# Cross-attention and gated FFN on one core: K, Q and V moved behind the first square layer, whose first three groups advance in step behind the gates

## The chip, the cores and the metric

The kernel runs on one core of a Trainium2 chip. Its five engines work side by side and meet at semaphores: TensorE (PE: matmuls, and PEld: the loading of their weights), VectorE (DVE), ScalarE (ACT), GpSimd (POOL) and SyncE (SP), which issues nearly all DMAs. The metric is the device time of one launch in microseconds (us), lower is better, as the median of several runs.

## The reference

32 sequences of 128 tokens, width 256, each with a context of 128 tokens of width 512.

```
xn  = layernorm(x)
kv  = (ctx @ W_src.T + b_src) * mask          # 512 -> 2*256: keys, values
q   = (xn  @ W_tgt.T + b_tgt) * mask          # 256 -> 256, 8 heads of 32
p   = softmax(where(mask, q @ k.T / sqrt(32), -inf))
x   = x + concat(xn, p @ v) @ W_out.T + b_out
h   = layernorm(x)
h   = silu((h @ w1.T) * s1) * ((h @ w2.T) * s2)   # 256 -> 1024, the gates
h   = gelu((h @ h1.T) * s3)                       # 1024 -> 1024, first square layer
h   = gelu((h @ h2.T) * s4)                       # 1024 -> 1024, second square layer
out = x + (h @ w3.T) * s5                         # 1024 -> 256
```

The weights of the FFN are whole numbers from -1 to 1. All data are float32.

## The kernel before, in words

**Tiles.** The 4096 tokens are cut into 16 tiles of two sequences (256 columns). Three tiles are under way at a time: while the FFN of tile f runs, tile a = f + 1 is in the second half of its attention (softmax normalised, transposed by a DMA round trip, weighted sums, output projection, second layer norm), tile n = f + 2 gets its K, Q, V and scores, and for tile m = f + 3 data are loaded and the first layer norm is done. Tile 0, and tiles 13, 14 and 15, are written out; tiles 1 to 12 are passes of a loop (`Fori`) that each engine has for itself. Each engine works through its own list in program order and waits at semaphores; there is no scheduler, so the order in which the helpers are called is the order of the work.

**Two operand halves.** The square layers and gates are computed as a high half (float32 rounded, "fp32r", line 780 in the square layers and 686 in the gates) and a low half (float16 with the high 16 bits of the weights, lines 778 and 685). Every activation is therefore split by DVE (`split`, lines 1379 to 1403) into `hAh`/`hAq` or `hBh`/`hBq`. K, Q, V, scores, weighted sums and output projection are plain float32 (lines 534, 552, 570, 588, 660, 677).

**PE's order in one pass f.** `gates_part` has four groups of gates (`gate_up`, q = 0 to 3, banks G0/G1 and F0/F1 in turn), then `project_k` twice, `project_q` and `project_v` of tile n. `middle_part` has the first square layer as q = 4 to 7 and the second as q = 8 to 11, in banks F0 and F1 in turn; each q has two halves of 128 output columns, and each half 8 high and 8 low products. Ahead of q = 8 stand `attend(a)`, `scores(n)` and `out_proj(a)`. Then comes `ffn_out`. In tiles 14 and 15 alone q = 4, 5, 6 are done by `middle_three`: the first halves of all three advance together, over k = 0 to 3, then 4 and 5, then 6 and 7, with the third group in G0, and the second halves follow. There the first square layer stands directly behind the gates, since no K, Q and V are left to compute.

**What feeds it.** ACT takes each gate bank through silu (`silu`, line 952), then has 16 exponentials of tile a, then the gelus (line 961) of q = 4 to 11. DVE multiplies gate by up (`gate_times_up`, line 1376), splits, adds bias and mask to K, Q and V (lines 1172, 1184, 1191), masks scores, normalises (1223), transposes 32 x 32 blocks (1277), and makes the two halves of the FFN's input from `x2T`: `x2h` by ACT and, in `x2_lo` (line 1343), the float16 `x2q` and a second low half `x2l`. `x2l` is read by PE only in a branch (`general`) for weights with low bits, which is not taken with these inputs. POOL has in tile 0 the rounding of the weights (`cast`, line 1623), which the second square layer of tile 0 waits for chunk by chunk, and the powers for the layer norms (1583, 1595).

**Tile 0** has an order of its own in DVE's list: `mask_scores(1, 0)` stands between `split(0, 0)` and `gate_times_up(0, 1)`, and the first layer norm of tile 3 (`ln1_apply`, which waits for POOL) stands ahead of `split(0, 10)`.

Of the kernel before, what the change touches and what calls it, by code (L numbers as in the profile page):

```python
# [12 lines left out]
NB = 2  # L13
# [30 lines left out]
def program(nc, x, ctxT, mask_row, mask_col, wsT, wvT, wtT, woT, first_rows, second_rows, x_mask_1, w1T, w2T, h1T, h2T,  # L44
            w3T, out):
    st = ExitStack()
    with st:
# [129 lines left out]
        def mid_bank(f, q):  # L177

            if q in (6, 10) and isinstance(f, int) and (f == TILES - 1 or f in (0, TILES - 2) and q == 6):
                return G[0][:].rearrange("p (h t) -> p h t", h=2)  # L180
            return F[q % 2][:]
# [172 lines left out]
        def _(sp):  # L354
# [43 lines left out]
            def turn_x2(a):  # L398
                sp.wait_ge(xt2_ready, at("xt2_ready", a - 1, 2))
                if not isinstance(a, int) or a > 1:  # L400
                    sp.wait_ge(x2T_loaded, at("x2T_loaded", a - 2, 64))
                sp.dma_start(x2_dram.rearrange("q p n -> p q n"), xt2[:].rearrange("p q c j i -> p q (c j i)")).then_inc(x2_written, 16)
                sp.wait_ge(x2_ready, at("x2_ready", a - 1, 2))
                sp.wait_ge(x2f_ready, at("x2f_ready", a - 1, 2))
                sp.wait_ge(x2_written, at("x2_written", a - 1, 16))
                for q in range(ROWS):
                    sp.dma_start(x2T[q * DH:(q + 1) * DH].rearrange("p a c j i -> p a (c j i)"),
                                 x2_dram[q].rearrange("(a b) n -> b a n", b=DH)).then_inc(x2T_loaded, 16)
# [14 lines left out]
            def tile(f, a, m):  # L423
                if m is not None:
                    load_ctx(m)
                    load_mask_row(m)
                if a is not None:
                    write_p(a, 0)
                    write_p(a, 1)
                    read_p(a, 0)  # L430
                    read_p(a, 1)
                if m is not None:
                    load_mask_col(m)
                    load_x(m)
                if a is not None:
                    turn_x2(a)
                if is_first(f):
                    spread_lift()
                if m is not None:
                    turn_x(m)  # L440
                store(f)
# [61 lines left out]
        def _(pe):  # L503
# [34 lines left out]
            def project_q(a, cs=range(KD), ks=range(KD)):  # L538
                by_dma = not isinstance(a, int) or a > 2
                if by_dma:  # L540
                    pe.wait_ge(xT_loaded, at("xT_loaded", a - 3, 64))
                    pe.wait_ge(sil_ready, at("sil_ready", a - 2, KH - 2))
                else:
                    pe.wait_ge(xnT_ready, at("xnT_ready", a, 1))
# [148 lines left out]

            def gate_group(bank, W, cols, lows, general):

                for low in lows:
                    for k in range(KD):
# [4 lines left out]
            def gate_up(f, q, general):  # L702

                gate_bank, up_bank = gate_banks(q)
                pe.wait_ge(x2_ready, at("x2_ready", f, 2))
                if general:
                    pe.wait_ge(x2f_ready, at("x2f_ready", f, 2))
                if q == 1 and isinstance(f, int) and f == 0:
# [5 lines left out]
                for h in range(2):  # L714
                    cols = slice((2 * q + h) * P, (2 * q + h + 1) * P)
                    ins = gate_group(gate_bank[:, h, :], (W1, W1_raw), cols, (h == 1, h == 0), general)
                ins.then_inc(gate_done, 1)
# [8 lines left out]
                for h in range(2):  # L726
                    cols = slice((2 * q + h) * P, (2 * q + h + 1) * P)
                    ins = gate_group(up_bank[:, h, :], (W2, W2_raw), cols, (h == 1, h == 0), general)
                ins.then_inc(up_done, 1)

            def middle_bank(f, q):
# [7 lines left out]
                elif q == 6 and isinstance(f, int) and f == 0:  # L739
                    pe.wait_ge(qT_ready, at("qT_ready", 2, 2))  # L740
                elif q == 6 and isinstance(f, int) and f >= TILES - 2:
                    pe.wait_ge(sil_ready, at("sil_ready", f, KH - 2))
                elif q == 7 and isinstance(f, int) and (f == 0 or f >= TILES - 2):
                    pe.wait_ge(gelu_ready, at("gelu_ready", f, 4))
                elif q == 8 and isinstance(f, int) and (f == 0 or f >= TILES - 2):
                    pe.wait_ge(gelu_ready, at("gelu_ready", f, 2))
# [89 lines left out]
            def gates_part(f, a, n, general):  # L836

                first = isinstance(f, int) and f == 0
                for q in range(4):
                    gate_up(f, q, general)  # L840
                    if first and q == 0:
                        scores(1)
                if n is not None:
                    if first:
                        transposes_x(2)
                    project_k(n, 0)
                    project_k(n, 1)
                    project_q(n)
                    project_v(n)

            def middle_part(f, a, n, general):

                first_scores = isinstance(f, int) and f in (0, TILES - 3)
                ends = isinstance(f, int) and f >= TILES - 2
                begun = isinstance(f, int) and f == 0
                for q in range(4, 12):
                    if q == 8 and begun:
                        second_layer_steps(range(KH // 2), general)
                    if q == 8 and first_scores:
                        scores(n)  # L860
# [4 lines left out]
                    if q == 8 and a is not None:  # L865
                        out_proj(a)
                    if ends and q < 7 or a is None and q in (8, 9, 10):
                        if q % 4 == 0:
# [263 lines left out]
        def _(dve):  # L1132
# [205 lines left out]
            def x2_lo(a):  # L1338
                dve.wait_ge(x2hi_ready, at("x2hi_ready", a, 2))
                dve.wait_ge(up_done, at("up_done", a - 1, 4))  # L1340
                for low, ready in ((x2q, x2_ready), (x2l, x2f_ready)):
                    for k in range(KD):
                        V.tensor_tensor(low[:, k, :].rearrange("p (j a i) -> p a j i", j=NB, a=ROWS), x2T[:, :, k],
                                        x2h[:, k, :].rearrange("p (j a i) -> p a j i", j=NB, a=ROWS).bitcast(F32),
                                        ALU.subtract).then_inc(ready, 1)

# [101 lines left out]
            def tile(f, a, n, m):  # L1448
# [6 lines left out]
                gate_times_up(f, 0)  # L1455
                split(f, 0)
                if first:
                    mask_scores(1, 0)
                gate_times_up(f, 1)
                if first:  # L1460
                    gate_times_up(f, 2)
# [14 lines left out]
                if first:  # L1476
                    row_max(1, 1)
                elif n is not None:
                    bias_mask_k(n)
                if n is not None:  # L1480
                    mask_bias(n)
                    bias_mask_q(n)
                if a is not None and not early:
                    normalise(a, 0)
                if n is not None and not first:
                    bias_v(n)
                if a is not None and not early:
# [6 lines left out]
                for q in range(4, 8):  # L1494
                    split(f, q)
                if n is not None:
                    mask_scores(n, 0)
# [13 lines left out]
                if m is not None:  # L1511
                    ln1_stats(m)
                    ln1_apply(m)
                elif n is not None:
                    normalise(n, 0)
                    turn_blocks(n, 0)
                split(f, 10)
                if m is not None:
# [227 lines left out]
```

## Time and profile before

| | |
|---|---|
| median of 3 runs | 896.8 us (896.63 to 896.85) |
| the profiled execution | 897.4 us |
| its span, first to last instruction | 895.6 us |
| granted TensorE clock, mean | 0.999 of full speed |
| PE busy | 889.3 us (99%), 7600 matmuls |
| PEld busy | 817.5 us (91%) |
| DVE busy | 655.5 us (73%) |
| ACT busy | 404.0 us (45%) |
| POOL busy | 79.8 us (9%) |
| DMA | 79.27 MB, mean 89 GB/s |

The profile is of one execution. The span leaves out 1.8 us around the first and the last instruction (897.4 - 895.6). Matmuls overlap in the array: one is shown for longer than the distance to the next, so a busy share of 99% says that PE had work, not how fast it went through it; for that one takes distances between starts, or the chain of waits, which lays the work end to end.

### The profile page before, as it was taken

How to read it: one execution, taken by the hardware profiler on the slowest of the kernel's cores; microseconds unless marked ns; L12 is line 12 of the kernel's file. 1: busy time of each engine (PE TensorE's matmuls, PEld its weight loads, DVE VectorE, ACT ScalarE, POOL GpSimd, SP SyncE). 2: the span in 40 equal slices, each digit the busy share in tenths (PEclk: the TensorE clock that was granted, in tenths of full speed). 3: DMA queues.
4: the chain of work that ended last, by engine and by line, in shares of the span. 5: the costliest groups of instructions: out<-in, count | busy, mean ns of one | idle time of the engine just before them, and what ended most of it. 6: DMA issues, size and time to landing. Idle time of an engine off the chain costs nothing.

```text
span 895.6 us, 20744 instructions
## 1 busy us (share of the span) xinstructions
PE 889.3 (99%) x7600; PEld 817.5 (91%) x7600; DVE 655.5 (73%) x1325; ACT 404.0 (45%) x1125; POOL 79.8 (9%) x109
## 2 busy tenths in 40 slices
PE   9999999999999999999999999999999999999998
PEld 8799899999999999999999999999999999998997
DVE  5897868678686886868768686786867868687463
ACT  5897624435244252533526235262443524455231
POOL 3545000010000100001010010100001000000000
PEclk9999999999999999999999999999999999999999
DMA  9932142412324122142321424113241222303000
GB/s 345 395 106 57 44 117 71 123 47 68 84 65 123 57 85 75 47 123 70 100 58 35 123 70 123 35 46 112 70 123 47 73 84 62 96 24 107 25 13 14
DMA packets 82498, 79.27 MB, mean 89 GB/s; under 512 B 8738, under 2 KB 75042, under 8 KB 82466
## 3 DMA queue, kind: packets, MB, share of 16 engines
q1 hardware_dynamic: 81890, 78.31, 28.2%
q10 hardware_dynamic: 576, 0.52, 0.2%
q8 instruction: 21, 0.34, 0.2%
q14 instruction: 11, 0.09, 0.0%
HBM read 51.55 MB, written 27.26 MB: 88 GB/s over the span
## 4 chain that ended last, share of the span: by engine, by line
PE 92%; DVE 3%; POOL 1%; issue 1%; DMA 1%; ACT 1%; SPq 0%; DVEq 0%; POOLq 0%
PE F L780 24%; PE F L778 22%; PE F L832 6%; PE G L677 6%; PE G L534 5%; PE G L570 5%; PE F L686 3%; PE G L686 3%; PE G L685 3%; PE F L685 3%; PE G L552 3%; PE S L588 2%; PE G L660 2%; PE F L692 1%; PE S L523 1%
## 5 line engine op out<-in xcount | busy, mean ns | idle before, releaser
L961 ACT ACTIVATE g<-F,small 128x256 f32<-128x256 f32 x118 | 49.6, 472 | 199.9 <-PE F L780 199.9
L780 PE MATMUL F<-hBh,H 128*128 128x256 f32 x944 | 131.5, 288 | 0.0
L780 PE MATMUL F<-hAh,H 128*128 128x256 f32 x928 | 130.7, 288 | 0.0
L780 PEld LDWEIGHTS F<-hBh,H 128*128 128x128 f32 x944 | 117.0, 188 | 1.7 <-ACT hBl_raw L961 0.3
L961 ACT ACTIVATE hBl_raw<-F,small 128x256 f32<-128x256 f32 x116 | 48.6, 472 | 155.0 <-PE F L780 155.0
L780 PEld LDWEIGHTS F<-hAh,H 128*128 128x128 f32 x928 | 115.3, 188 | 1.9 <-ACT hAl_raw L952 0.4
L778 PE MATMUL F<-hBq,H 128*128 128x256 f16 x944 | 114.4, 273 | 0.0
L778 PE MATMUL F<-hAq,H 128*128 128x256 f16 x928 | 113.5, 273 | 0.0
L778 PEld LDWEIGHTS F<-hBq,H 128*128 128x128 bf16 x944 | 87.3, 98 | 11.9
L778 PEld LDWEIGHTS F<-hAq,H 128*128 128x128 bf16 x928 | 85.4, 98 | 11.7
L1398 DVE TENSOR_SCALAR hBl_raw<-hBl_raw,small 128x512 f32<-128x512 f32 x60 | 29.2, 486 | 87.3 <-ACT hBl_raw L961 87.3
L988 ACT ACTIVATE pr<-pr,nmx 128x128 f32<-128x128 f32 x240 | 92.6, 387 | 0.5 <-DVE nmx L1216 0.3
L1595 POOL TENSOR_TENSOR rs<-ve,neg_half 128x2 f32<-128x2 f32 x15 | 10.5, 702 | 639.2 <-DVE ve L1326 639.2
L832 PE MATMUL F<-W,hAh 128*128 128x256 f32 x256 | 61.7, 282 | 1.0 <-DVE hAl L1402 0.9
L832 PE MATMUL F<-W,hAl 128*128 128x256 f32 x256 | 61.5, 281 | 0.0
L686 PE MATMUL F<-x2h,W 128*128 128x256 f32 x256 | 51.5, 302 | 0.6 <-DVE g L1376 0.6
L686 PE MATMUL G<-x2h,W 128*128 128x256 f32 x256 | 51.2, 301 | 0.0
L534 PE MATMUL G<-cT,WK 128*128 128x256 f32 x224 | 50.7, 379 | 0.0
L570 PE MATMUL G<-WV,cT 128*128 128x256 f32 x224 | 50.6, 379 | 0.0
L952 ACT ACTIVATE hAl_raw<-G,gscols 128x256 f32<-128x256 f32 x60 | 25.2, 471 | 55.2 <-PE G L686 55.2
L832 PEld LDWEIGHTS F<-W,hAh 128*128 128x128 f32 x256 | 48.3, 189 | 1.4 <-DVE hAl L1402 1.4
L1402 DVE TENSOR_TENSOR hAl<-g,hAh 128x512 fp32r<-128x512 f32 x68 | 47.1, 693 | 2.3
(209 smaller groups left out, 1659.2 us busy)
## 6 DMA issues: line engine op xcount, KB each, us to landing
p_dram<-pb SPq DMA_DIRECT2D x30, 512.0 KB, 3.3
pr<-p_dram SPq DMA_DIRECT2D x120, 128.0 KB, 3.2
H_raw<-h SPq DMA_DIRECT2D x16, 512.0 KB, 13.9
cT<-ctx_t SPq DMA_DIRECT2D x14, 512.0 KB, 3.2
x_dram<-xt SPq DMA_DIRECT2D x28, 256.0 KB, 2.3
out<-y SPq DMA_DIRECT2D x32, 128.0 KB, 1.7
x_in<-x_t SPq DMA_DIRECT2D x15, 256.0 KB, 2.7
x2T<-x_dram SPq DMA_DIRECT2D x60, 64.0 KB, 1.9
```

Source lines behind the costliest of these rows:

```text
L534: ins = mm(k_part(a, c), WK[:, k, c * P:(c + 1) * P], cT_of(a)[:, k, :], start=k == 0, stop=k == KC - 1)
L570: ins = mm(v_bank(a)[:, j * D:(j + 1) * D], cT_of(a)[:, k, j * P:(j + 1) * P], WV[:, k, :], start=k == 0, stop=k == KC - 1)
L677: ins = mm(G[1][:, j * D:(j + 1) * D], lhsT, WO[:, k, :], start=k == 0, stop=k == 2 * KD - 1)
L685: return mm(bank, high_halves(W[0])[:, k, cols], x2q[:, k, :], start=first, stop=last)
L686: return mm(bank, W[0][:, k, cols], x2h[:, k, :], start=first, stop=last)
L778: ins = mm(bank, high_halves(W[0])[:, k, cols], low16[:, k, :], start=first, stop=last)
L780: ins = mm(bank, W[0][:, k, cols], hi[:, k, :], start=first, stop=last)
L832: ins = mm(F[j][:, 0, :], lhsT, W3[:, k, :], start=first, stop=last)
L961: fn(g_pair(f, q)[:, m, :], mid_bank(f, q)[:, m, :], ACT.Gelu, scale=scale).then_inc(gelu_ready, 1)
L988: ins = fn(pr[j][:, r, c, :], pr[j][:, r, c, :], ACT.Exp, bias=nmx[:, j, h:h + 1], scale=SCALE, accum_out=den[:, j, h:h + 1])
L1398: V.tensor_scalar(whole_g, whole_g, lift[:, 1:2], None, ALU.mult).then_inc(in_lift, 1)
L1402: V.tensor_tensor(lo[:, pair, :], whole_g, hi[:, pair, :].bitcast(F32), ALU.subtract).then_inc(h_ready, 1)
```

## The change

1. PE: `project_k`, `project_q` and `project_v` of tile n leave `gates_part` and stand ahead of `attend`, behind q = 7, for every tile but 0.
2. PE: `middle_three` is used for q = 4, 5, 6 in tiles 1 to 13 too; q = 6 is in bank G0 in every tile. The waits on banks follow: q = 6 waits for the silu of q = 2, q = 7 for gelu of 5, q = 8 for gelu of 4, and `project_q` for gelu of 6.
3. DVE: the bias and mask steps of K, Q and V stand behind the splits of q = 4 to 7. The second low half `x2l` is no longer made outside tile 0; the branch that read it multiplies the whole `x2T` instead.
4. DVE, tile 0: `gate_times_up(0, 1)` stands ahead of `mask_scores(1, 0)`, and `split(0, 10)` ahead of `ln1_apply(3)`.
5. SP: the loads of context and mask row of tile m stand behind the DMAs of `p` (outside tile 0).

```diff
@@ mid_bank
-            if q in (6, 10) and isinstance(f, int) and (f == TILES - 1 or f in (0, TILES - 2) and q == 6):
+            if q == 6 or q == 10 and isinstance(f, int) and f == TILES - 1:
                 return G[0][:].rearrange("p (h t) -> p h t", h=2)
@@ SP, turn_x2
-                sp.wait_ge(x2f_ready, at("x2f_ready", a - 1, 2))
+                sp.wait_ge(up_done, at("up_done", a - 1, 4))
@@ SP, tile
-                if m is not None:
+                if is_first(f):
                     load_ctx(m)
                     load_mask_row(m)
...
                     read_p(a, 0)
                     read_p(a, 1)
+                if m is not None and not is_first(f):
+                    load_ctx(m)
+                    load_mask_row(m)
@@ PE, project_q
-                    pe.wait_ge(sil_ready, at("sil_ready", a - 2, KH - 2))
+                    pe.wait_ge(gelu_ready, at("gelu_ready", a - 2, 6))
@@ PE, gates (the branch that is not taken with these inputs)
+            def whole_group(bank, W, cols):
+
+                to = bank.rearrange("p (j a i) -> p j a i", j=NB, a=ROWS)
+                for k in range(KD):
+                    ins = mm(to, W[1][:, k, cols], x2T[:, :, k].rearrange("p a j i -> p j a i"), start=k == 0, stop=k == KD - 1)
+                return ins
...
+                if general and not is_first(f):
+                    return whole_group(bank, W, cols)
@@ PE, middle_bank
-                elif q == 6 and isinstance(f, int) and f >= TILES - 2:
+                elif q == 6:
                     pe.wait_ge(sil_ready, at("sil_ready", f, KH - 2))
-                elif q == 7 and isinstance(f, int) and (f == 0 or f >= TILES - 2):
+                elif q == 7:
                     pe.wait_ge(gelu_ready, at("gelu_ready", f, 4))
-                elif q == 8 and isinstance(f, int) and (f == 0 or f >= TILES - 2):
+                elif q == 8:
                     pe.wait_ge(gelu_ready, at("gelu_ready", f, 2))
@@ PE, gates_part
-                if n is not None:
-                    if first:
-                        transposes_x(2)
-                    project_k(n, 0)
-                    project_k(n, 1)
-                    project_q(n)
-                    project_v(n)
+                if first:
+                    transposes_x(2)
+                    project(2)
+
+            def project(n):
+
+                project_k(n, 0)
+                project_k(n, 1)
+                project_q(n)
+                project_v(n)
@@ PE, middle_part
+                    if q == 8 and n is not None and not begun:
+                        project(n)
...
-                    if ends and q < 7 or a is None and q in (8, 9, 10):
+                    if not begun and q < 7 or a is None and q in (8, 9, 10):
                         if q % 4 == 0:
                             middle_three(f, q, general)
@@ DVE, x2_lo
-                for low, ready in ((x2q, x2_ready), (x2l, x2f_ready)):
-                    for k in range(KD):
...
+                for k in range(KD):
+                    V.tensor_tensor(x2q[:, k, :].rearrange("p (j a i) -> p a j i", j=NB, a=ROWS), x2T[:, :, k],
+                                    x2h[:, k, :].rearrange("p (j a i) -> p a j i", j=NB, a=ROWS).bitcast(F32),
+                                    ALU.subtract).then_inc(x2_ready, 1)
@@ DVE, tile
                 split(f, 0)
+                gate_times_up(f, 1)
                 if first:
                     mask_scores(1, 0)
-                gate_times_up(f, 1)
-                if first:
                     gate_times_up(f, 2)
...
-                elif n is not None:
-                    bias_mask_k(n)
-                if n is not None:
                     mask_bias(n)
                     bias_mask_q(n)
...
-                if n is not None and not first:
-                    bias_v(n)
...
                 for q in range(4, 8):
                     split(f, q)
+                if n is not None and not first:
+                    bias_mask_k(n)
+                    mask_bias(n)
+                    bias_mask_q(n)
+                    bias_v(n)
...
                     ln1_stats(m)
+                    if first:
+                        split(f, 10)
                     ln1_apply(m)
...
-                split(f, 10)
+                if not first:
+                    split(f, 10)
```

## Rows read from the trace of the kernel before

**Rows 1.** The page, part 1: busy time of each engine, share of the span.

```profile
PE 889.3 (99%) x7600; PEld 817.5 (91%) x7600; DVE 655.5 (73%) x1325; ACT 404.0 (45%) x1125; POOL 79.8 (9%) x109
```

**Rows 2.** Busy time by stretch, one pass of the loop (PE, PEld, DVE, ACT, POOL).

```profile
367.68:422.38 54.70, 54.70 (x474) 50.49 (x473) 40.87 (x83) 22.93 (x66) 2.85 (x4) 1.00 0.27 79
```

**Rows 3.** The chain of waits, same pass: start us, us, what.

```profile
375.09 3.45 PE G L534 x16
378.54 1.73 PE G L552 x8
...
383.72 0.93 PE F L780 x8
...
398.26 1.01 PE G L660 x32
399.27 1.10 PE S L588 x32
```

**Rows 4.** Timeline of PE, same pass: start us, us, what [idle before].

```profile
374.61 0.48 PE L686 MATMUL F<-x2h,W 128*128 128x256 f32 x2
...
398.19 1.08 PE L660 MATMUL G<-pr,v 128*32 128x128 f32 x32
```

**Rows 5.** Timeline of PE, tile 14, from the gates' end to `attend`.

```profile
812.20 0.48 PE L686 MATMUL F<-x2h,W 128*128 128x256 f32 x2
...
827.65 0.64 PE L660 MATMUL G<-pr,v 128*32 128x128 f32 x16
```

**Rows 6.** Timeline of PEld, tile 15, at the gates' end.

```profile
858.62 0.53 PEld L780 LDWEIGHTS F<-hAh,H 128*128 128x128 f32 x4 [0.21 <-ACT hAl_raw L952]
```

**Rows 7.** Timeline of DVE, the pass of rows 2.

```profile
378.58 0.88 DVE L1172 SCALAR_TENSOR_TENSOR kT<-G,firsts 128x256 f32<-128x256 f32 x2 [0.37 <-PE G L534]
...
383.92 0.69 DVE L1191 TENSOR_TENSOR vb<-G,firsts 128x512 f32<-128x512 f32 x1 [1.37 <-PE G L570]
...
400.76 1.22 DVE L1208 TENSOR_TENSOR pr<-S,mbias 128x1024 f32<-128x1024 f32 x1
```

**Rows 8.** Timeline of ACT, same pass.

```profile
382.63 1.28 ACT L961 ACT_TABLE_LOAD   x1
387.39 0.84 ACT L961 ACTIVATE hBl_raw<-F,small 128x256 f32<-128x256 f32 x2 [3.48 <-PE F L780]
```

**Rows 9.** Timeline of DVE, tile 0, about the last splits.

```profile
87.04 0.17 DVE L1149 TENSOR_SCALAR ve<-mv 128x2 f32<-128x2 f32 x1
88.04 0.74 DVE L1158 TENSOR_SCALAR xn<-x_in,mv,rs 128x256 f32<-128x256 f32 x2 [0.83 <-POOL rs L1583]
...
89.14 0.69 DVE L1402 TENSOR_TENSOR hAl<-g,hAh 128x512 fp32r<-128x512 f32 x1
...
91.08 0.75 DVE L1343 TENSOR_TENSOR x2l<-x2T,x2h 128x256 fp32r<-128x256 f32 x2
91.75 0.42 DVE L1400 CAST hAh<-g 128x512 fp32r<-128x512 f32 x1
```

**Rows 10.** Timeline of PE, tile 0.

```profile
88.69 0.28 PE L832 MATMUL F<-W,hAh 128*128 128x256 f32 x1
...
92.95 0.39 PE L832 MATMUL F<-W,hAh 128*128 128x256 f32 x1 [0.90 <-DVE hAl L1402]
...
93.99 0.39 PE L686 MATMUL G<-x2h,W 128*128 128x256 f32 x2
```

**Rows 11.** Timeline of PE, tile 0, fourth group of gates and the second square layer's first steps.

```profile
42.75 0.50 PE L686 MATMUL F<-x2h,W 128*128 128x256 f32 x2 [0.55 <-DVE g L1376]
...
68.50 0.38 PE L692 MATMUL F<-hBh,H 128*128 128x256 f32 x1
```

**Rows 12.** Timeline of ACT, tile 0: the last exponential.

```profile
58.83 0.19 ACT L988 ACTIVATION_READ_ACCUMULATOR pr<-pr,nmx 128x1 f32 x1
```

**Rows 13.** Timeline of DVE, tile 0: what follows it.

```profile
59.37 0.18 DVE L1220 RECIPROCAL rden<-den 128x8 f32<-128x8 f32 x1
```

**Rows 14.** Timeline of POOL, tile 0: roundings of the second square layer's weights.

```profile
63.25 3.74 POOL L1623 CAST H<-H_raw 128x1024 fp32r<-128x1024 f32 x3 [10.36 <-issue]
```

More of the change, by code:

```diff
@@ L692, in part_product, with gate_group @@
                 return mm(bank, W[0][:, k, cols], part[:, k, :], start=first, stop=last)
-            def gate_group(bank, W, cols, lows, general):
+            def whole_group(bank, W, cols):
[3 more added lines that the diff above has]
+                return ins
+            def gate_group(f, bank, W, cols, lows, general):
+                if general and not is_first(f):
+                    return whole_group(bank, W, cols)
                 for low in lows:
@@ L705, in gate_up @@
                 pe.wait_ge(x2_ready, at("x2_ready", f, 2))
-                if general:
-                    pe.wait_ge(x2f_ready, at("x2f_ready", f, 2))
+                if general and is_first(f):
+                    pe.wait_ge(x2f_ready, 2)
                 if q == 1 and isinstance(f, int) and f == 0:
@@ L715, in gate_up @@
                     cols = slice((2 * q + h) * P, (2 * q + h + 1) * P)
-                    ins = gate_group(gate_bank[:, h, :], (W1, W1_raw), cols, (h == 1, h == 0), general)
+                    ins = gate_group(f, gate_bank[:, h, :], (W1, W1_raw), cols, (h == 1, h == 0), general)
                 ins.then_inc(gate_done, 1)
@@ L727, in gate_up @@
                     cols = slice((2 * q + h) * P, (2 * q + h + 1) * P)
-                    ins = gate_group(up_bank[:, h, :], (W2, W2_raw), cols, (h == 1, h == 0), general)
+                    ins = gate_group(f, up_bank[:, h, :], (W2, W2_raw), cols, (h == 1, h == 0), general)
                 ins.then_inc(up_done, 1)
@@ L842, in gates_part @@
                         scores(1)
-                if n is not None:
-                    if first:
-                        transposes_x(2)
-                    project_k(n, 0)
-                    project_k(n, 1)
-                    project_q(n)
-                    project_v(n)
+                if first:
[6 more added lines that the diff above has]
+                project_v(n)
             def middle_part(f, a, n, general):
                 first_scores = isinstance(f, int) and f in (0, TILES - 3)
-                ends = isinstance(f, int) and f >= TILES - 2
                 begun = isinstance(f, int) and f == 0
@@ L1340, in x2_lo @@
                 dve.wait_ge(up_done, at("up_done", a - 1, 4))
-                for low, ready in ((x2q, x2_ready), (x2l, x2f_ready)):
-                    for k in range(KD):
-                        V.tensor_tensor(low[:, k, :].rearrange("p (j a i) -> p a j i", j=NB, a=ROWS), x2T[:, :, k],
-                                        x2h[:, k, :].rearrange("p (j a i) -> p a j i", j=NB, a=ROWS).bitcast(F32),
-                                        ALU.subtract).then_inc(ready, 1)
+                for k in range(KD):
+                    V.tensor_tensor(x2q[:, k, :].rearrange("p (j a i) -> p a j i", j=NB, a=ROWS), x2T[:, :, k],
+                                    x2h[:, k, :].rearrange("p (j a i) -> p a j i", j=NB, a=ROWS).bitcast(F32),
+                                    ALU.subtract).then_inc(x2_ready, 1)
             def turn_x(a):
```

## Prediction

> **What bounds the kernel now.** I read in this order: the busy shares, one pass of the loop by stretch, the chain of waits through that pass, the timelines at the seams that the change moves, and tiles 0, 14 and 15.
>
> PE is busy for 99% of the span, DVE for 73% [rows 1]. A matmul's busy time overlaps with the next, so the share alone proves little. The stretch of one pass says more: a pass is 54.70 us from gates to gates, and in it PE has no idle time at all, DVE works 40.87 us and ACT 22.93 us [rows 2]. In the chain of waits the same pass is an unbroken row of PE pieces that start where the last one ended (the ends of it: [rows 3]): gates end at 375.09, K takes 3.45, Q 1.73, V ends at 383.72, the first square layer at 398.26. PE's 99% over the span [rows 1] leaves no room for passes of another kind, and 13 tiles (1 to 13) have this order of work. So between about 94 us and the end of tile 13 no wait sets the pace; PE's own work does. A change of order there can remove nothing, since it removes no product that is computed with these inputs. It can only add: a wait, or a costlier sequence of products. What can be gained is in tile 0, where PE does wait.
>
> **The loop: K, Q and V behind q = 7, the three groups in step behind the gates.** These go together. The products are the same, 8.63 us of K, Q and V (383.72 - 375.09) and 14.54 us of first square layer (398.26 - 383.72) [rows 3]; only their seams change. Before, 8.63 us of K, Q and V stood between the last gates and q = 4, and covered the last silu and two splits. After, that cover is gone. What is late then is to be seen in tiles 14 and 15, which already have this order: PE's weight loads stood idle 0.21 us for ACT's last silu [rows 6].
>
> The whole price comes from tile 14. Its last pair of gate products starts at 812.20 and `attend` at 827.65, 15.45 us apart [rows 5]. The loop's own numbers say what this would be without loss: the chain's end of the gates (375.09) lies 0.48 us behind the start of the last pair (374.61), and attend's chain start (398.26) 0.07 us behind its start (398.19) [rows 3, 4]; so 0.48 + 14.54 - 0.07 = 14.95 us. The difference is 0.50 us. About 0.2 of it is the silu; the other 0.3 is the order itself, in which runs of 4 or 2 high products alternate with as many low ones, where before there were runs of 8 and 16. Thirteen tiles change to this order: 13 x 0.50 = +6.5 us.
>
> I take tile 14's number because the code is the same and the silu stands the same in both. Bounds per tile: 0.2 if only the silu's wait comes along (the alternation is then a peculiarity of one tile), 0.7 if the waits in the loop, whose values are counted in registers, add as much again as the silu's. Below nothing I exclude: there is no idle time to win [rows 2].
>
> The Trainium skill has a rule that speaks against the 0.3: "TensorE: Matmul & The Clock Gate", section "Back-to-back issue gap", gives one distance per matmul by its columns (256 columns, some 109 ns), whatever stands beside it. By that the order would cost nothing and the loop 0.2 us a tile; this is the first rival below. This case's trace does not agree: tile 14 lost 0.50, more than twice the idle time that its weight loads show.
>
> **The other seams.** Each new wait has a slack, counted from the gates' end E = 375.09 (after: first square layer until E + 15.0, K until 18.5, Q until 20.2, V until 23.7):
> - q = 7 (at E + 11.4) needs the gelus of q = 5 out of F1. ACT's exponentials end at 382.63, E + 7.54; the table load takes 1.28, to 8.8; q = 4 is ready for gelu by about E + 8 (64 of the products of 0.114 us, with the 0.5 of delay); two gelu pairs of 0.84 [rows 8] end at 10.6, or with the wait for q = 5 at 10.7. Slack 0.7.
> - V (E + 20.2) needs K out of G1. DVE's last split used to end at 400.76, 2.5 us behind the end of q = 7 [rows 3, 7], so now at E + 17.5; K's two steps start when K is done, 18.5, and take 0.9 [rows 7]. Slack 0.8.
> - `attend` (E + 23.7) needs Q out of G0: done by 21.2. `out_proj` stands 2.1 us behind `attend` (1.01 + 1.10) [rows 3] and needs V's bias, 0.69 us from the end of V [rows 7]. Slack 1.4.
> - The second square layer needs the splits of q = 4 to 7, which end at E + 17.5, and starts behind `out_proj`, near E + 29.5: more slack than before.
> - SP: context and mask row now wait behind V (E + 23.7), and `p`'s DMAs are ahead of them, free sooner, since DVE's normalising no longer has the bias steps among it. Queued behind are the mask column, x and `x2T`, all wanted later than that. Context is needed a pass later.
>
> I take all of these at nothing. If one slack is used up, the price is what it is overrun by, 13 times (the second rival).
>
> The half `x2l` is 0.67 us of DVE per tile (91.08 to 91.75 in tile 0) [rows 9], in 13 tiles where PE waits for nothing: worth 0. The multiplication of the whole `x2T` is in a branch that is not taken: 0. This part of the change does nothing here.
>
> **Tile 0.** Two places.
>
> The last split. PE begins `ffn_out` at 88.69 and the next gates at 93.99, 5.30 us for 32 products. It idled for DVE's `hAl` until 92.95, 0.90 us shown [rows 10]. The last 8 products took 93.99 - 92.95 = 1.04, so 32 at the pace of the other steps are about 3.8 (the 0.12 us of the loop's 117 ns each, 8 in 0.93 [rows 3]). DVE's side: after the statistics (ready 87.21) it waited 0.83 us for POOL, did `ln1_apply`, and only then `split(0, 10)`, which ended at 89.83; transposes and `x2_lo` followed, `x2l` as 0.67 of it, then the last split from 91.75 [rows 9]. With `split(0, 10)` ahead, its 1.1 us lie over POOL's 0.83, and `x2l` is gone: 0.83 + 0.67 = 1.5 us sooner, the last split ends at about 91.4. PE wants it at 88.69 + 24 x 0.117 = 91.5. So the wait ends and the gates start at 88.69 + 3.8 = 92.5: -1.5 us. Bounds: -1.0 (only the idle time shown) to -1.6 (5.30 - 3.7).
>
> `gate_times_up(0, 1)` ahead of `mask_scores`. PE idled 0.55 us for it ahead of 42.75 [rows 11]. That goes, but is it kept? At 68.50 PE runs into the rounding of the second square layer's fourth chunk by POOL (the stretched product of [rows 11]). POOL starts that series at 63.25 and needs more than 1.2 us for each (3.74 for 3) [rows 14], behind `p` of tile 1, which DVE makes behind ACT's exponentials. Those ended at 59.02, ACT-bound; DVE took up at 59.37 [rows 12, 13]. So of the 0.55 only those 0.35 can come through. I take -0.4, rounded up; bounds 0 to -0.7.
>
> **Sum.** +6.5 - 1.5 - 0.4 = +4.6 us. On the profiled execution, 897.4, that makes 902.0. The median of the runs is 896.8, 0.6 below, so I forecast 901.4.
>
> **The rivals.**
> 1. The order costs nothing, only the silu's wait remains (the skill's rule above): 13 x 0.2 = 2.6, less 1.9: +0.7, 897.5. For it: each piece of the alternation is small. Against: tile 14's 0.50 is a plain difference of starts. 6%.
> 2. A further wait in every pass. The tightest are gelu of q = 5 (0.7) and K's bias (0.8); if DVE or ACT runs 1.1 behind, 0.3 to 0.5 a pass are added, 4 to 6 us: 906. For it: both slacks are below a single 128 x 1024 step of DVE (1.22 [rows 7]). Against: such a step stands at neither place. 9%.
> 3. The other side, faster than before: in the loop the silu ends in time and the alternation is hidden by the weight loads, which work 50.49 of 54.70 us [rows 2], so that only tile 0's gain is left: 896.8 - 1.9 = 894.9. It turns at 1.9 / 13 = 0.15 us a tile. Against: tiles 14 and 15 show the wait. 3%.
>
> The Trainium skill, "ScalarE: Activation LUTs", section "What ACT_TABLE_LOAD costs", speaks for this rival: it counts 1.38 us of drain to the 1.28 us of the load. The rows show the 1.28, and not whether a drain follows, since the gelu behind it waited for PE. With the page's drain the gelu of q = 5 would end near E + 11.9, 0.5 behind the need, and the sum would come to 6.5 us more.
>
> **How the numbers follow.** Forecast 82%, rivals 6, 9 and 3%. The forecast's own range is 13 x (0.4 to 0.6) less 1.2 to 2.3, +2.9 to +6.6: 899.7 to 903.4. For 8 in 10 I widen it by 0.7 below and 1.4 above for the slacks: 899.0 to 904.8. A change within 0.2% (1.8 us, 895.0 to 898.6) could not be told from none. Faster 3%, same 6%, slower 91%.
>
> **What would show it.** A pass of about 55.2 us; between the last gates and `middle_three` PEld idle some 0.2 us for ACT L952 in every tile; no PE wait ahead of K, V, `attend` or `out_proj`; gates of tile 1 starting near 92.1 instead of 93.99, with no wait for `hAl`. I am wrong if the pass is still 54.7, or if a wait longer than 0.2 us stands in it.

## The result, and the profile after

| | before | after |
|---|---|---|
| median of the runs | 896.83 us (4 runs) | 902.58 us (902.4 to 902.85, 4 runs) |
| ratio, 95% interval | | 1.0064 (1.0052 to 1.0076) |
| span of the profiled execution | 895.6 us | 900.7 us |
| one pass of the loop | 54.70 us | 55.28 us |
| start of tile 1's gates | 93.99 us | 91.81 us |

The change costs 5.75 us, 0.64%; forecast were +4.6, and 902.58 lies within the range of 899.0 to 904.8. The page of the changed kernel, part 1, looks like the one of before [rows 1]:

```profile
PE 894.7 (99%) x7600; PEld 814.1 (90%) x7600; DVE 647.8 (72%) x1295; ACT 404.3 (45%) x1125; POOL 79.9 (9%) x109
```

The same number of matmuls, 5.4 us more of PE's busy time, 30 steps and 7.7 us less of DVE's, which bought nothing. That a share of 99% stays 99% while the kernel gets slower is the first thing to see. One pass, as a stretch (window, length, then PE, PEld, DVE, ACT, POOL), against [rows 2]:

```profile
364.58:419.86 55.28, 55.20 (x475) 50.33 (x474) 40.33 (x80) 22.86 (x66) 2.84 (x4) 1.00 0.27 78
```

PE is shown idle for 0.08 us of it, where the pass is 0.58 longer. The rest is booked as busy time and has to be looked for in the chain of waits. That chain, from the end of the gates to the end of the first square layer:

```profile
375.78 0.09 issue
375.87 0.73 PE F L792 x4
376.60 0.45 PE F L790 x4
377.05 0.52 PE F L792 x4
377.57 0.46 PE F L790 x4
378.03 0.47 PE G L792 x4
378.50 0.45 PE G L790 x4
378.96 0.24 PE F L792 x2
...
381.80 0.87 PE F L790 x8
...
387.27 0.93 PE F L792 x8
...
390.91 3.45 PE G L537 x16
394.36 1.73 PE G L555 x8
396.09 3.45 PE G L573 x16
399.54 1.01 PE G L663 x32
...
401.65 3.65 PE G L680 x16
```

(L792 and L790 are the high and low products, 780 and 778 before; one line of the chain is called a piece here.) The three groups take 387.27 - 375.87 = 11.40 us, where three groups of 14.54 / 4 = 3.635 us [rows 3] took 10.90. The four products behind the silu take 0.73 us, those of the third group 0.47. From q = 7 on every piece follows the last at once: K, Q and V take 8.63 us as before, `attend` starts at their end. PE has no stall at any seam behind the first one. PEld is shown idle there once more, 0.33 us ahead of `attend` (4.0 us in 12 over the span), but experiment 3 below has this too, and its pass is only 0.03 us longer than that of experiment 1, which has not. At that first seam PEld shows what it waits for in the loop:

```profile
375.86 0.53 PEld L792 LDWEIGHTS F<-hAh,H 128*128 128x128 f32 x4 [0.28 <-issue]
```

In tile 15 before, the same step had 0.21 and named ACT's silu [rows 6]; in the loop it has 0.28 and names nothing. The timeline of ACT has the silu's end at 374.90 + 0.84 = 375.74, 0.12 ahead of the weight load:

```profile
374.90 0.84 ACT L968 ACTIVATE hAl_raw<-F,gscols 128x256 f32<-128x256 f32 x2 [1.01 <-PE F L689]
...
383.34 1.28 ACT L977 ACT_TABLE_LOAD   x1
384.64 1.68 ACT L977 ACTIVATE hBl_raw<-F,small 128x256 f32<-128x256 f32 x4
```

The last row holds the gelus of q = 4 and 5, done at 386.32, 0.95 ahead of q = 7 (387.27). They begin 0.02 behind the end of the table load (383.34 + 1.28 = 384.62). The drain of 1.38 us, which "ScalarE: Activation LUTs" of the Trainium skill (section "What ACT_TABLE_LOAD costs") adds to a load, does not stand between them. The other two close seams, from DVE's timeline of the same pass (last split of the first layer, K's bias, V's bias; before: [rows 7]):

```profile
392.80 0.69 DVE L1417 TENSOR_TENSOR hBq<-hBl_raw,hBh 128x512 f16<-128x512 f32 x1
394.40 0.88 DVE L1188 SCALAR_TENSOR_TENSOR kT<-G,firsts 128x256 f32<-128x256 f32 x2 [0.91 <-PE G L537]
...
399.58 0.69 DVE L1207 TENSOR_TENSOR vb<-G,firsts 128x512 f32<-128x512 f32 x1 [2.58 <-PE G L573]
```

K's bias ends at 395.28, 0.81 ahead of V's start in the chain (396.09); V's ends at 400.27, 1.38 ahead of `out_proj` (401.65).

In tile 0 PE's timeline has no wait left ahead of the last products, and the gates of tile 1 follow 3.83 us behind the start of `ffn_out`, where it was 5.30 [rows 10]:

```profile
87.98 0.28 PE L844 MATMUL F<-W,hAh 128*128 128x256 f32 x1
...
90.81 0.34 PE L844 MATMUL F<-W,hAh 128*128 128x256 f32 x1
...
91.81 0.39 PE L689 MATMUL G<-x2h,W 128*128 128x256 f32 x2
```

### The profile page after: what moved, and what is told of

It reads as the page before. It is cut to its first block, busy times and chain, and to the rows that moved or that the text cites. A ratio compares the mean times of both kernels' runs of the same rounds, so it can differ in the third digit from the quotient of the medians.

```text
span 900.7 us, 20738 instructions
## 1 busy us (share of the span) xinstructions
PE 894.7 (99%) x7600; PEld 814.1 (90%) x7600; DVE 647.8 (72%) x1295; ACT 404.3 (45%) x1125; POOL 79.9 (9%) x109
## 4 chain that ended last, share of the span: by engine, by line
PE 94%; DMA 2%; DVE 2%; ACT 1%; issue 1%; SPq 0%; POOL 0%; DVEq 0%; POOLq 0%
PE F L792 22%; PE F L790 20%; PE F L844 7%; PE G L680 6%; PE G L537 6%; PE G L573 5%; PE G L689 3%; PE F L689 3%; PE G L688 3%; PE F L688 3%; PE G L792 3%; PE G L790 3%; PE G L555 2%; PE S L591 2%; PE G L663 2%; PE F L695 2%
## 5 line engine op out<-in xcount | busy, mean ns | idle before, releaser
L792 PE MATMUL F<-hBh,H 128*128 128x256 f32 x944 | 131.5, 288 | 0.0
L792 PE MATMUL F<-hAh,H 128*128 128x256 f32 x720 | 120.4, 296 | 1.0
L792 PEld LDWEIGHTS F<-hBh,H 128*128 128x128 f32 x944 | 117.0, 188 | 1.7 <-ACT hBl_raw L977 0.3
L790 PE MATMUL F<-hBq,H 128*128 128x256 f16 x944 | 114.4, 273 | 0.0
L790 PE MATMUL F<-hAq,H 128*128 128x256 f16 x720 | 102.0, 274 | 0.0
L792 PEld LDWEIGHTS F<-hAh,H 128*128 128x128 f32 x720 | 94.4, 189 | 6.2 <-issue 3.4
L790 PEld LDWEIGHTS F<-hBq,H 128*128 128x128 bf16 x944 | 87.3, 98 | 12.0
L790 PEld LDWEIGHTS F<-hAq,H 128*128 128x128 bf16 x720 | 60.9, 98 | 10.6
L1049 ACT ACTIVATE upd<-G 128x512 f32<-128x512 f32 x15 | 9.0, 598 | 119.0 <-PE G L663 107.6
L977 ACT ACTIVATE hBl_raw<-F,small 128x256 f32<-128x256 f32 x90 | 37.4, 472 | 42.1 <-PE F L792 42.0
L1415 DVE CAST hAh<-g 128x512 fp32r<-128x512 f32 x68 | 29.6, 435 | 35.2 <-ACT g L977 35.2
L1224 DVE TENSOR_TENSOR pr<-S,mbias 128x1024 f32<-128x1024 f32 x30 | 36.6, 1221 | 19.8 <-PE S L591 17.4
```

The lines of the kernel that those rows point to most:

```text
L790: ins = mm(bank, high_halves(W[0])[:, k, cols], low16[:, k, :], start=first, stop=last)
L792: ins = mm(bank, W[0][:, k, cols], hi[:, k, :], start=first, stop=last)
L977: fn(g_pair(f, q)[:, m, :], mid_bank(f, q)[:, m, :], ACT.Gelu, scale=scale).then_inc(gelu_ready, 1)
L1224: V.tensor_tensor(pr[j][:], S[:, :, j, :, :], bias, ALU.add).then_inc(masked, 1)
L1415: V.tensor_copy(hi[:, pair, :], whole_g).then_inc(hi_ready, 1)
```

## The experiments

Each was timed beside the kernel before: its median was 897.0 us beside the first four and 896.9 beside the rest. Differences to the changed kernel compare medians of separate sessions, in which the kernel before agreed within 0.15 us. The difference of two medians has no interval of its own; those of the ratios reach about 0.1% (0.9 us) to either side. Small effects are therefore read from the traces, by the length of a pass, and only the total from the times.

### 1. The three groups in step, nothing moved

The kernel before, with the step order of the change in tiles 1 to 13 too. K, Q and V stay ahead of it and cover the silu. The waits on banks follow from q = 6 being in G0, where Q was; the one with `a - 1, 6` is `attend`'s.

```diff
-            if q in (6, 10) and isinstance(f, int) and (f == TILES - 1 or f in (0, TILES - 2) and q == 6):
+            if q == 6 or q == 10 and isinstance(f, int) and f == TILES - 1:
...
+                    pe.wait_ge(gelu_ready, at("gelu_ready", a - 1, 6))
...
+                elif q == 6:
+                    pe.wait_ge(qT_ready, at("qT_ready", f + 2, 2))
-                elif q == 7 and isinstance(f, int) and (f == 0 or f >= TILES - 2):
+                elif q == 7:
...
-                elif q == 8 and isinstance(f, int) and (f == 0 or f >= TILES - 2):
+                elif q == 8:
...
-                    if ends and q < 7 or a is None and q in (8, 9, 10):
+                    if not begun and q < 7 or a is None and q in (8, 9, 10):
```

> The kernel before with the first square layer's groups q = 4, 5, 6 in step in tiles 1 to 13 (q = 6 in bank G0), and nothing else: K, Q and V stay behind the gates, tile 0 is untouched. My theory, that the alternation of short runs of high and low products costs 0.3 us a tile and the silu's wait 0.2 to 0.3 more: here K, Q and V cover the silu, so only the alternation is left, 13 x 0.3 = +4 us against the kernel before, a pass of 55.0 us with no PE wait. The rival, that order costs nothing and all of the loss is waiting at the seam: no change, within 1 us, a pass of 54.7.

Measured: 898.89 us, ratio 1.0016 (1.0007 to 1.0025), 1.9 more. One pass by stretch, and the chain of waits at the step order's start:

```profile
364.72:419.58 54.86, 54.86 (x475) 50.43 (x474) 40.92 (x84) 22.90 (x66) 2.84 (x4) 1.00 0.27 79
```

```profile
384.55 0.46 PE F L783 x4
385.01 0.45 PE F L781 x4
385.46 0.47 PE F L783 x4
385.93 0.45 PE F L781 x4
386.39 0.47 PE G L783 x4
```

The pass is 0.16 longer than the 54.70 of [rows 2], without any idle time. The first high pieces take 0.46 and 0.47 us, where the changed kernel has 0.73 and 0.52: these two belong to the silu. So the order by itself costs something, which the first rival denied, but half of the 0.3 that I gave it. The written-out tile 13 shows the same: 54.85 us, +0.15.

### 2. K, Q and V moved, the square layer group by group

The changed kernel, with the banks, the waits and the order of the first square layer as they were.

```diff
-            if q == 6 or q == 10 and isinstance(f, int) and f == TILES - 1:
+            if q in (6, 10) and isinstance(f, int) and (f == TILES - 1 or f in (0, TILES - 2) and q == 6):
...
-                elif q == 6:
+                elif q == 6 and isinstance(f, int) and f >= TILES - 2:
                     pe.wait_ge(sil_ready, at("sil_ready", f, KH - 2))
-                elif q == 7:
+                elif q == 7 and isinstance(f, int) and (f == 0 or f >= TILES - 2):
...
-                elif q == 8:
+                elif q == 8 and isinstance(f, int) and (f == 0 or f >= TILES - 2):
...
-                    if not begun and q < 7 or a is None and q in (8, 9, 10):
+                    if isinstance(f, int) and f >= TILES - 2 and q < 7 or a is None and q in (8, 9, 10):
```

> The changed kernel with the first square layer of tiles 1 to 13 in its old order (q = 4, 5, 6 one after another, in F0 and F1), so that K, Q and V are moved but the three groups don't advance in step. Theory: q = 4 alone reaches products k = 4 to 7 some 0.8 us behind the gates, while DVE's splits of q = 2 and 3 end 1.3 to 3.0 us behind them; PE waits for the silu and twice for a split, 1.8 us a pass, 13 x 1.8 = 23 us, less the 2 us won in tile 0: about 918 us, a pass of 56.5. The rival, that the step order buys nothing because the splits are early enough: 898 us or less, below the changed kernel by the 4 us of alternation.

Measured: 932.88 us, ratio 1.0392 (1.0376 to 1.0409); a pass takes 57.43 us. PEld's waits over the span (what waits, for what: sum in us, count, mean):

```profile
PEld F L792 <- DVE hAh L1415: 20.1, 26, 0.8
PEld F L792 <- ACT hBl_raw L977: 7.5, 12, 0.7
PEld G L663 <- issue: 4.0, 12, 0.3
PEld F L792 <- issue: 3.4, 12, 0.3
```

The two waits for a split, 20.1 us in 26 over 13 tiles, were expected. The wait for a gelu was not, and the time came out 15 us above the 918 expected. In this order q = 6 goes into F0 again and wants q = 4 out of it, while ACT still has the exponentials and the table load ahead of that gelu (chain of waits):

```profile
393.14 1.34 ACT pr L1004 x7
394.48 0.02 issue
394.50 1.28 ACT L977
395.78 0.01 issue
395.80 0.85 ACT hBl_raw L977 x2
396.64 0.04 issue
396.69 1.20 PE F L792 x8
```

The pass grew by 57.43 - 54.70 = 2.73, where 1.8 was expected. So the step order and the third bank, at 0.16 us, save 57.43 - 55.28 = 2.15 us a pass once the cover is gone: the two parts of the change only make sense together.

### 3. The group whose bank is free goes first

The changed kernel; only the order inside the step changes, and the waits for splits go to the group that leads. q = 6 uses G0, whose wait (for the gates' silu of that bank) was met long before; q = 4 is the one that waits for the last silu.

```diff
                 three = (q, q + 1, q + 2)
+                order = (q + 2, q, q + 1) if q == 4 else three
                 for ks in (range(4), (4, 5), (6, 7)):
-                    for i in three:
+                    for i in order:
                         if ks[0] == 0:
                             middle_bank(f, i)
-                        middle_steps(f, i, 0, ks, general)
+                        middle_steps(f, i, 0, ks, general, i == order[0])
```

> The changed kernel with the groups of the three first halves in the order q = 6, 4, 5: q = 6 is in G0, whose silu is done a group of gates earlier, so PE has 0.9 us of work before it needs the last silu's bank. The semaphore waits for the splits go to q = 6. Theory: the 0.28 us that the weight loads stand idle for in each of tiles 1 to 15 vanish, -15 x 0.25 = -3.8 us against the changed kernel, about 898.8 us, a pass of 55.0. The rival, that this idle time is the cost of the sequencer's register waits and not the silu's: no more than 0.5 us won.

Measured: 897.16 us, ratio to the kernel before 0.9998 (0.9989 to 1.0007), 5.4 us below the changed kernel. One pass by stretch, and the chain of waits behind the gates:

```profile
363.55:418.44 54.89, 54.89 (x475) 50.28 (x474) 40.34 (x80) 22.70 (x66) 2.84 (x4) 1.00 0.27 79
```

```profile
374.52 0.24 PE F L689 x2
374.76 0.47 PE G L797 x4
375.22 0.45 PE G L795 x4
375.68 0.47 PE F L797 x4
```

The idle time of PEld at this line is gone in the loop, the first piece takes 0.47, and a pass is 0.39 us shorter (55.28 - 54.89), where the idle time shown was 0.28. The difference can be read off the changed kernel's chain: 0.09 between its last gates (375.78) and the first piece (375.87), 0.26 that this piece took more (0.73 - 0.47), 0.05 for the one after the next (0.52 - 0.47), together 0.40. So most of what the late weight load costs is booked as busy time of the products behind it, and not as idle time.

### 4. Every second piece turned around

The changed kernel; nine times a group advances over some k, with high products and then low ones, and every second time it now takes the low ones first. Like kinds (high, low) meet, and the kind changes eight times fewer.

```diff
                     lows = (half == 1, half == 0)
+                    if turned_lows:
+                        lows = lows[::-1]
...
-                        middle_steps(f, i, 0, ks, general)
+                        middle_steps(f, i, 0, ks, general, i == order[0], n % 2 == 1)
+                        n += 1
```

> The changed kernel with the order of high and low turned in every second piece of the three first halves (high low, low high, high low, ...), so that neighbouring pieces join: some 8 changes of kind fewer per tile, the same products, the same waits. Theory: about half of the alternation's 0.3 us goes, -15 x 0.1 to 0.15 = -1.5 to -2.3 us against the changed kernel, about 900.6 us, the silu's idle time unchanged. The rival, that the loss is not in the changes of kind: no difference.

Measured: 900.39 us, ratio 1.0033 (1.0021 to 1.0046), 2.2 us below the changed kernel. One pass by stretch, and the chain of waits from the end of the gates:

```profile
363.78:418.92 55.14, 55.06 (x475) 50.34 (x474) 40.34 (x80) 22.69 (x66) 2.84 (x4) 1.00 0.27 78
```

```profile
375.06 0.73 PE F L799 x4
375.79 0.89 PE F L797 x8
376.68 0.48 PE F L799 x4
377.16 0.46 PE G L799 x4
...
380.85 0.87 PE F L797 x8
```

PEld's idle time at the silu stays what it was (3.4 us in 12). The pass is 0.14 us shorter (55.28 - 55.14), nearly experiment 1's 0.16, but that is not eight changes alone: the chain has to be taken in two parts. From the third group's first piece on, the same 32 products take 380.85 - 377.16 = 3.69 us with 7 changes of kind, where the changed kernel has 14 and takes 381.80 - 378.03 = 3.77: 0.08 / 7, about 0.01 us for each. The other 0.06 lies ahead of that, in the pieces behind the silu (2.10 us instead of 2.16), with one change fewer and 0.48 where 0.52 stood. Experiment 1 gives the same price: in its three groups the kind changes 22 times instead of 6, and 0.16 / 16 is 0.01 us. So the changes between fp32r and float16 products account for the whole cost of the order; the changes of bank, which are left in here, need no price.

### 5. Without `x2l`

The kernel before; the low half for the branch that is not taken is no longer made outside tile 0.

```diff
-                for low, ready in ((x2q, x2_ready), (x2l, x2f_ready)):
-                    for k in range(KD):
...
+                for k in range(KD):
...
```

> The kernel before without the second low half x2l outside tile 0, and nothing else (its branch for weights with low bits, which is not taken, multiplies the whole x2T). Theory: DVE's two steps of x2l take 0.67 us; in the loop PE waits for nothing and they are worth 0, in tile 0 they stand in the chain to the last split, so the gates of tile 1 start 0.6 us sooner: -0.6 us, pass 54.70. The rival, that DVE's load slows the passes: -0.6 us a pass, -8 us in all.

Measured: 896.29 us, ratio 0.9991 (0.9982 to 1.0). From `ffn_out` (88.25) to the gates of tile 1 (92.88) it takes 4.63 us, where it was 5.30 [rows 10]: 0.67 less, and the total is 0.6 less, at the edge of what its interval tells from none. DVE has 30 steps fewer (1295), two for each of 15 tiles, and where PE has no wait they bought nothing: the twelve passes of the loop take 656.45 us (92.88 to 749.33), before 656.42 (93.99 to 750.41).

### 6. The split ahead of the norm

The kernel before; in tile 0 `split(0, 10)` stands ahead of `ln1_apply(3)`.

```diff
                     ln1_stats(m)
+                    if first:
+                        split(f, 10)
                     ln1_apply(m)
...
-                split(f, 10)
+                if not first:
+                    split(f, 10)
```

> The kernel before with split(0, 10) ahead of ln1_apply(3) in tile 0, and nothing else. Theory: the split fills the 0.83 us in which DVE waits for POOL, the last split ends 0.8 us sooner and the stall of 0.90 us ahead of ffn_out's last products nearly closes: -0.8 us. With x2l's 0.6 this gives 1.4 to 1.5, the gain of the changed kernel in that stretch. The rival, that the layer norm of tile 3 is then late: no gain, or a wait at K, Q, V of tile 3.

Measured: 896.16 us, ratio 0.9995 (0.9986 to 1.0004), by itself not told from none. The stretch of `ffn_out` (87.95 to 92.47) is 4.52 us, 0.78 shorter, and 0.47 of the wait is left (PE's timeline):

```profile
91.42 0.39 PE L832 MATMUL F<-W,hAh 128*128 128x256 f32 x1 [0.47 <-DVE hAl L1402]
```

0.67 and 0.78 make 1.45; the changed kernel, which has both, is 5.30 - 3.83 = 1.47 shorter. They add.

### 7. `gate_times_up` ahead of `mask_scores`

The kernel before; in tile 0 the second group's product of gate and up comes first.

```diff
-                if first:
-                    mask_scores(1, 0)
                 gate_times_up(f, 1)
                 if first:
+                    mask_scores(1, 0)
                     gate_times_up(f, 2)
```

> The kernel before with gate_times_up(0, 1) ahead of mask_scores(1, 0) in tile 0, and nothing else. What I forecast: PE's 0.55 us at the fourth group of gates vanishes, 0.35 to 0.4 of it is kept. The rival, from the changed kernel's trace, where weighted sums of tile 1 waited for the DMA of p: all of it is lost there, 0 us (within 0.15).

Measured: 896.79 us, ratio 1.0001 (0.9992 to 1.001). The wait ahead of the fourth gates is gone, and the time did not change measurably. PE's timeline shows what took its place:

```profile
68.56 0.39 PE L692 MATMUL F<-hBh,H 128*128 128x256 f32 x1
...
70.98 0.64 PE L660 MATMUL G<-pr,v 128*32 128x128 f32 x16 [0.24 <-DMA pr<-p_dram]
```

The two profiles start tile 0 differently (see "Tile 0" in the section on the prediction), so I count from DVE's first low half, `hAl`, which starts at 40.46 here and at 40.09 before. The fourth chunk of the rounded weights is then ready 28.10 us behind it, before 28.41 [rows 11]: 0.31 sooner, where the forecast had 0.35. But halfway through `attend` PE waits for the DMA of `p`, which I had not looked at, and `out_proj` starts 31.10 us behind that mark, before 31.04. All of it is lost in this execution.

It is not lost in every one. The same distance is 31.12 in the changed kernel, where PE waits 0.25 for the same DMA, but 30.79, 30.76 and 30.86 in experiments 2, 3 and 4, which have the same tile 0 and show no such wait; without the edit it is 31.00 to 31.35 (experiments 1, 5 and 6, and the kernel before). So the edit keeps between nothing and 0.3 us, and the landing of that DMA decides how much. What moves the landing no run isolates.

### 8. What the runs point to

K, Q and V stay where they were in the loop. Kept are the three edits of tile 0 and, in tiles 14 and 15, where the groups advance in step anyway, q = 6 first and turned pieces.

```diff
+                order = (q + 2, q, q + 1) if q == 4 and True else three
+                n = 0
                 for ks in (range(4), (4, 5), (6, 7)):
...
+                        middle_steps(f, i, 0, ks, general, i == order[0], n % 2 == 1)
+                        n += 1
```

> The kernel before in its order (K, Q, V behind the gates, square layer group by group), with the three edits of tile 0 and the two that the first runs pointed to, where groups advance in step anyway: tiles 14 and 15 begin with q = 6, and every second piece of three first halves has high and low turned. Theory: -1.5 us for the last split of tile 0, 0 to -0.4 for its gates, 2 x -0.36 for the silu's wait, 3 x -0.12 for the changes of kind: -2.6 to -3.0 us, 894.2. The rival, that these small gains don't add because tile 14 waits for the DMA of p anyway: about -1.9.

Measured: 894.23 us (893.94 to 894.4), ratio 0.997 (0.9958 to 0.9983): 2.7 us below the kernel before, 8.4 (902.58 - 894.23) below the changed one, and faster than both. That it meets the 894.2 is partly luck, as the trace shows by its parts. From the same mark in tile 0 to the gates of tile 1 it is 52.13 us instead of 53.90: 1.77 saved, which is 1.47 for the last split and 0.30 more, as in the profiles above where the DMA of `p` lands in time. Tile 15 saves 0.51 (43.88 us from its gates to the end, before 44.39). Tile 14 saves only 0.07 (45.86, before 45.93), where some 0.5 was expected: `attend` starts 0.39 sooner, but then waits for the DMA of `p`, 0.61 us where it was 0.29, so the rival was right for that tile.

```profile
825.99 0.64 PE L660 MATMUL G<-pr,v 128*32 128x128 f32 x16 [0.61 <-DMA pr<-p_dram]
```

Together that is 2.35 us, where the medians differ by 2.7.

## Why the prediction was right, point by point

**What bounds the kernel.** Right. Experiment 5 took 0.6 us of DVE out of every pass and moved only tile 0; each 0.1 us on PE's chain in the loop came back twelve times.

**+0.50 a tile, from tile 14.** The place was right and the size a little low. The changed kernel's written-out tile 13 takes 55.21 us where it took 54.70 (chain, gates to tile 14's gates: 755.33 to 810.54, before 750.58 to 805.28), +0.51 and so exactly the term. The twelve passes of the loop take +0.58 each. 12 x 0.58 + 0.51 = 7.5, where the sum had 6.5: this mis-sized term is most of what lies between 901.4 and 902.58. The rest of the account is -1.47 for tile 0's last split and -0.14 in tile 14 (45.79 us, before 45.93), where the wait of 0.29 us for the DMA of `p` is gone, which I had not foreseen: +5.9, measured +5.75. Tile 14 stood in straight code; in the loop the weight load comes 0.12 us behind the silu's end, in tile 14 0.05. That the excess of the loop belongs to this wait is shown: experiment 3, where PE does not meet it, has 54.89 us in the loop and 54.90 in tile 13, and experiment 1 has 54.86 and 54.85. The waits in the loop compare with values counted in registers, the only difference that I know of. I had that as the reason for the upper bound of 0.7; that it is the reason is argued and not shown, since no run isolates it.

**Its two parts.** Wrong, and hidden by their sum. I gave the silu 0.2 and the order 0.3; experiments 3 and 1 give 0.39 and 0.16. The step that failed is "about 0.2 of it is the silu": I took the 0.21 us of idle time shown for the price of the wait, and removing the wait brought 0.39 where 0.28 was shown. Since the order's share was formed as the rest, the one mistake made the other. Taken from the difference of starts, the sum was safe from both. My sign of being wrong, a wait longer than 0.2 us in the pass, was badly set for the same reason: PEld shows 0.28 at the silu, PE 0.08, and neither is the 0.39 that the wait costs.

**The first rival, that the order costs nothing.** Fell: the interval of experiment 1 leaves out zero, and experiment 4 takes half of the changes of kind out of a stretch and saves 0.08 us of it. I had this rival from the Trainium skill, "TensorE: Matmul & The Clock Gate", section "Back-to-back issue gap", and read too much into it: the 109 ns for 256 columns follow from the gap that it gives for an isolated matmul. For a stream it says that weight load and matmul together set the spacing. The section names no price for a change of kind, so the 0.16 us do not contradict it.

**The other seams at nothing.** Right. Slacks of 0.7, 0.8 and 1.4 were forecast for the gelu of q = 5, K's bias and V's bias; 0.95, 0.81 and 1.38 were found. The second rival fell with them, and so did the sum with a drain behind the table load, which was this rival's and not the third's, as the place of that paragraph could suggest.

**The third rival, only tile 0's gain.** Fell: 0.58 is well over its turning point of 0.15. Experiment 3 shows how near it lay all the same: with another group first, the kernel is level with the one before.

**Tile 0.** The last split was to bring -1.5 and brought -1.47 (0.67 + 0.78). The product ahead of `mask_scores` was to bring -0.4. In the changed kernel it kept nothing that can be read, in others up to 0.3 (experiment 7); I had counted ACT and DVE up to `p`, and not the DMA round trip behind it. The changed kernel's gates of tile 1 start 2.18 us sooner (91.81 against 93.99), which looks like more than 1.47, but 0.79 of it is there in DVE's first split of tile 0 already (39.30 against 40.09), before any of the edits acts. That start lies anywhere from 39.30 to 40.60 in the profiles of the kernels here (40.60 in experiment 3, 39.81 in 1, 39.31 in 8), so absolute starts of two profiles are not to be compared, distances within one are.

## What to carry to other kernels

Where the critical engine has no idle time in its steady passes, a new order of the same work can hardly win there and can cost, and what can be gained lies at the ends. Price a new order from a place in the same trace that already has it, by differences of starts and not by idle times shown: 0.28 us shown cost 0.39 here, and starting with the group whose bank is free took it away. A stall that is removed early is worth only what the next late resource leaves of it, so follow that one through its DMAs too.

## What the runs showed of the hardware

- A change between fp32r and float16 products costs PE about 0.01 us, an average of many: 16 more of them make a pass 0.16 us longer (54.86 against 54.70, experiment 1), and 7 fewer make the same 32 products 0.08 us shorter (3.69 against 3.77, experiment 4).
- ACT's table load takes 1.28 us, and the next activation starts 0.02 us behind it (384.62 to 384.64 in the changed kernel). In experiment 2 the load starts 0.02 us behind the last exponential (394.48 to 394.50), so nothing stands ahead of it either.
- A weight load that comes late costs more than the idle time shown: 0.28 us shown, 0.39 us saved without it (experiment 3).
- The granted clock stays near full speed through short waits: its mean is 0.996 even in experiment 2, where PEld waits up to 0.8 us, twice for a split and once each for a gelu and the silu in a pass.
